# First attention: score banks 3 to 4, maxima banks 4 to 3, one exp per two score tiles

## The reference

```
def _L0_attn_ref(x, w_qkv, b_qkv, w_o, b_o):
    ...
    attn = jax.nn.softmax(jnp.einsum('blhc,bmhc->bhlm', q, k) * SCALE, axis=-1)
    heads = jnp.einsum('bhlm,bmhc->blhc', attn, v).reshape(b, l, d)
    return jnp.einsum('bld,ed->ble', heads, w_o) + b_o + x
...
    x = L0_attn_x
    xn = _layernorm(x, axis=-1)
    s = _L0_attn_ref(xn, ...)
    g = _silu(_L0_ffn_ref(xn, ...))
    x = x + s * g
```

## Time and profile before

| | us |
|---|---|
| median of 3 runs | 2436.63 |
| lowest, highest | 2425.33, 2439.51 |
| the profiled execution's own time | 2435.27 |
| its span in the trace | 2433.4 |
| first reduction of maxima to the last (L1026) | 226.8 to 1589.4 |

### The profile page before, as it was taken

How to read it: one execution, slowest core, us unless ns; L and a number is a source line. 1 busy time by engine, 2 the same in 40 slices (tenths; PEclk the granted TensorE clock), 3 DMA queues, 4 the chain that set the end, 5 groups by cost and what they waited for, 6 DMA issues and landing times. The chain is left out here.

```text
span 2433.4 us, 43647 instructions
## 1 busy us (share of the span) xinstructions
PE 2212.6 (91%) x14912; PEld 1228.7 (50%) x14912; DVE 1839.2 (76%) x3240; ACT 1442.7 (59%) x2160; POOL 462.6 (19%) x673
## 2 busy tenths in 40 slices
PE   7896899999999999999999999988999987899988
PEld 4664333333333333333333333326888876666678
DVE  5664999999999999999999999912444466888745
ACT  3443377777777777777777777772222222366743
POOL 0000000000000000000000000003545520366745
PEclk9997699999999999999999999989999999688999
DMA  6888400500500501403205002006576459766664
GB/s 206 283 288 183 53 6 6 62 6 8 62 3 13 57 3 26 44 6 44 26 3 64 6 8 62 3 3 176 154 186 157 135 190 373 170 145 146 154 164 130
DMA packets 189129, 231.90 MB, mean 95 GB/s; under 512 B 72720, under 2 KB 122768, under 8 KB 186064
## 3 DMA queue, kind: packets, MB, share of 16 engines
q1 hardware_dynamic: 176048, 210.46, 35.3%
q10 hardware_dynamic: 7184, 14.10, 2.7%
q0 software_dynamic: 5728, 5.00, 0.9%
HBM read 138.97 MB, written 89.13 MB: 94 GB/s over the span
## 5 line engine op out<-in xcount | busy, mean ns | idle before, releaser
L1026 DVE TENSOR_REDUCE a_maxes<-a_ps_a 128x2 f32<-128x1024 f32 x1024 | 1202.2, 1221 | 114.3 <-PE a_ps_a L1147 110.5
L1091 ACT ACTIVATE a_prob<-a_ps_s 128x512 f32<-128x512 f32 (+1 forms) x1376 | 1035.7, 804 | 355.2 <-PE a_ps_s L1173 349.5
L1173 PE MATMUL a_ps_s<-a_Q,a_K 50*128 50x512 f32 x2048 | 596.3, 455 | 89.8 <-ACT a_prob L1091 89.6
L1147 PE MATMUL a_ps_a<-a_K,a_Q 48*128 48x512 f32 x2048 | 551.9, 455 | 26.0 <-DMA a_Q<-s_halves 14.4
L1185 PE MATMUL a_ps_o<-a_prob,a_V 128*17 128x512 f32 x4096 | 544.9, 604 | 0.1
L1173 PEld LDWEIGHTS a_ps_s<-a_Q,a_K 50*128 50x128 f32 x2048 | 278.4, 186 | 508.7 <-ACT a_prob L1091 459.7
L1147 PEld LDWEIGHTS a_ps_a<-a_K,a_Q 48*128 48x128 f32 x2048 | 245.8, 189 | 231.5 <-issue 107.9
L984 POOL DMA_DIRECT2D a_Q<-a_m_parts x128 | 64.3, 503 | 1286.9 <-DVE a_m_parts L1018 1280.3
L1593 DVE CUSTOM_DVE_ANT_0 a_scratch<-a_ps_a,k_mask 128x256 f32<-128x256 f32 (+1 forms) x512 | 178.0, 411 | 25.9 <-PE a_ps_a L1710 24.0
L1653 ACT ACTIVATE a_prob<-a_ps_s 128x512 f32<-128x512 f32 (+1 forms) x256 | 135.6, 583 | 98.8 <-PE a_ps_s L1746 97.3
L1185 PEld LDWEIGHTS a_ps_o<-a_prob,a_V 128*17 128x17 f32 x4096 | 68.0, 95 | 150.9 <-issue 99.0
(11 more groups left out here) (195 smaller groups left out, 2260.2 us busy)
## 6 DMA issues: line engine op xcount, KB each, us to landing
s_halves<-p_parts SPq DMA_DIRECT2D x32, 512.0 KB, 5.1
s_halves<-k_K SPq DMA_DIRECT2D x32, 512.0 KB, 7.7
a_Q<-s_halves SPq DMA_DIRECT2D x186, 64.0 KB, 10.5
a_K<-s_halves SPq DMA_DIRECT2D x42, 256.0 KB, 9.0
s_xT<-p_xT SPq DMA_DIRECT2D x32, 256.0 KB, 4.0
s_cT<-p_cT SPq DMA_DIRECT2D x32, 256.0 KB, 3.7
k_wb<-s_w SPq DMA_DIRECT2D x16, 512.0 KB, 7.7
c_wb<-s_w SPq DMA_DIRECT2D x16, 512.0 KB, 8.1
```

The source lines that it names most:

```text
L1026: nc.vector.tensor_reduce(maxes[:, :, slot, qt, kc], ps_a[:, o:o + 2 * CH].rearrange("p (z k) -> p z k", z=2), AX.X, ALU.max).then_inc(a_d ...
L1091: nc.scalar.activation(prob[:, ring:ring + len(t), :].rearrange("p r q -> p (r q)"), ps_s[:, bank:bank + len(t) * CH], ACT.Exp, scale=scal ...
L1147: last = nc.tensor.matmul(ps_a[:, o + side * CH:o + (side + 1) * CH], Q[rows, q0:q0 + P], K[rows, k0:k0 + CH], start=True, stop=True)
L1173: last = nc.tensor.matmul(ps_s[:, bank + x * CH:bank + (x + 1) * CH], K[rows, k0:k0 + P], Q[rows, q0:q0 + CH], start=True, stop=True)
```

## The change

`ps_s` gets four banks and `ps_a` three. Every score step is now two tiles in two banks with one exp over 128x1024, 32 steps per iteration instead of 43. The maxima are taken in slots: an even slot is two tiles with a reduction of 128x1024, an odd slot one tile with a reduction of 128x512; an iteration has 44 slots, one of which (32) is the turn, so 21 pairs and 22 singles where there were 32 units. A slot waits for the one two before it, which used the same banks. `through(it, i)` counts the finished reductions for these waits, `slot_due` places the slots on the made-up clock by the tiles that lie before them, and the value steps are due a little later (`LAG` 30, was 24). `maxes` is now laid out in the order of the tiles. The prologue takes chunk 0 in 43 slots, and the early slots after it are 13 reductions more, with the turn between them. The copy of the output on ScalarE comes behind exp 3, which ends tile 7, where it came behind exp 2, which ended tile 4.

```
-    NJ = 2 * (TILES_IT // 3) + 1
-    NU = PAIR * TT * NCH
-    EARLY = 9
-    NPOS = NU + 1
-    TURN = NU - EARLY + 2
+    NJ = TILES_IT // 2
+    NTILES = PAIR * TT * NCH * 2
+    SLOTS = 44
+    TURN = 32
+    LAST = TURN - 3
+    EARLY = 19
+    FIRST_SLOTS = 43
...
     def tiles_of(j):
-        t = 3 * (j // 2) + (2 if j % 2 else 0)
-        return [t, t + 1] if j % 2 == 0 and t + 1 < TILES_IT else [t]
+        return [2 * j, 2 * j + 1]
...
     def clock_of(j):
-        return 12 * ((j + 1) // 2) + 7 * (j // 2)
+        return 12 * j
     ROUND = clock_of(NJ)
-    UNIT_LAG, LAG, LATE, COPY_AT = 1, 24, 1, 2
-    def unit_due(p):
-        return p * ROUND / NPOS + UNIT_LAG if p < NPOS else 2 * ROUND
+    LAG, LATE, COPY_AT = 30, 2, 3
+    def before_slot(i):
+        return 3 * (i // 2) + (2 if i % 2 else 0)
+    def bank_of(i):
+        return 2 * CH if i % 2 else 0
+    def slot_due(i):
+        return before_slot(i) * ROUND / before_slot(SLOTS) if i < SLOTS else 2 * ROUND
+    def slot_at(i):
+        first = EARLY + before_slot(i) - (2 if i > TURN else 0)
+        return 1 + first // NTILES, first % NTILES, 1 if i % 2 else 2
+    def first_slot_at(i):
+        x = before_slot(i)
+        return x, min(1 if i % 2 else 2, NTILES - x)
+    def through(it, i):
+        return (SLOTS - 1) * (it + 1) + FIRST_SLOTS - (TURN - 2) + (i if i < TURN else i - 1) + 1
...
-        maxes = n.sb("maxes", [P, 2, PAIR, TT, NCH])
+        maxes = n.sb("maxes", [P, NTILES])
-        ps_a = n.ps("ps_a", 4 * CH)
-        ps_s = n.ps("ps_s", 3 * CH)
+        ps_a = n.ps("ps_a", 3 * CH)
+        ps_s = n.ps("ps_s", 4 * CH)
...
-            def maximum(c, k, o):
-                slot, qt, kc = k // (TT * NCH), (k // NCH) % TT, k % NCH
+            def maximum(c, x, count, o, done):
...
-                dve.wait_ge(a_ready, NU * c + k + 1)
-                nc.vector.tensor_reduce(maxes[:, :, slot, qt, kc],
-                                        ps_a[:, o:o + 2 * CH].rearrange("p (z k) -> p z k", z=2), AX.X, ALU.max
+                dve.wait_ge(a_ready, done)
+                nc.vector.tensor_reduce(maxes[:, x:x + count],
+                                        ps_a[:, o:o + count * CH].rearrange("p (z k) -> p z k", z=count), AX.X, ALU.max
                                         ).then_inc(a_done, 1)
...
-            def bank_free(it, p):
-                passed_by = p - 1 - (1 if TURN <= p - 2 else 0)
-                pe.wait_ge(a_done, 2 + NU * (it + 1) + EARLY + passed_by)
+            def bank_free(it, i):
+                if it < 0 and i < TURN:
+                    pe.wait_ge(a_done, FIRST_SLOTS)
+                elif i >= 2:
+                    pe.wait_ge(a_done, through(it, i - 2))
+                else:
+                    pe.wait_ge(a_done, through(it - 1, SLOTS + i - 2))
```

More of the change, by code:

```diff
@@ L1045, in normalise, with iteration @@
                                         ).then_inc(o_done, 1)
[L1047 to L1051, removed]
+            def iteration(it, more):
+                for i in range(SLOTS):
+                    if i == TURN:
+                        split_maxima(it + 1, bank_of(i))
+                        normalise(it, bank_of(i))
                         continue
-                    step, k = unit_at(p)
+                    step, x, count = slot_at(i)
                     if step == 1 or more:
-                        maximum(it + step, k, bank_of(parity, p))
-                    if k == NU - 1:
-                        whole_maxima(it + 1)
+                        maximum(it + step, x, count, bank_of(i), through(it, i))
+                    if i == LAST:
+                        whole_maxima(it + 1, through(it, i))
             nc.vector.memset(ps_o[:], 0.0).then_inc(o_clear, 1)
-            dve.sem_inc(a_done, 2)
             dve.sem_inc(o_done, 1)
@@ L1063, in _ @@
             dve.wait_ge(router_step, 7)
[L1064 to L1069, removed]
-                else:
[L1071 to L1077, removed]
+            for i in range(FIRST_SLOTS):
+                maximum(0, *first_slot_at(i), bank_of(i), i + 1)
+            whole_maxima(0, FIRST_SLOTS)
+            for i in range(TURN - 2, SLOTS):
+                if i == TURN:
+                    split_maxima(0, bank_of(i))
+                else:
+                    maximum(1, *slot_at(i)[1:], bank_of(i), through(-1, i))
+            with dve.Fori(0, NIT - 2) as it:
+                iteration(it, True)
+            iteration(NIT - 2, False)
+            for it in (NIT - 1, NIT):
+                normalise(it, bank_of(TURN))
         @block.scalar
@@ L1130, in _, with maximum_scores @@
         def _(pe):
-            def bank_of(r, p):
-                return ((1 + r + p) % 2) * 2 * CH
-            def bank_free(it, p):
-                passed_by = p - 1 - (1 if TURN <= p - 2 else 0)
-                pe.wait_ge(a_done, 2 + NU * (it + 1) + EARLY + passed_by)
-            def maximum_scores(c, r, k, o):
-                slot, qt, kc = k // (TT * NCH), (k // NCH) % TT, k % NCH
+            def bank_free(it, i):
[5 more added lines that the diff above has]
+                    pe.wait_ge(a_done, through(it - 1, SLOTS + i - 2))
+            def maximum_scores(c, r, x, count, o):
                 half, qc = ((r // NCH) % 2) * LONG, r % NCH
-                for side in range(2):
+                for y in range(count):
+                    k, side = (x + y) // 2, (x + y) % 2
+                    slot, qt, kc = k // (TT * NCH), (k // NCH) % TT, k % NCH
                     rows = slice(side * SIDE, side * SIDE + HALF_ROWS)
@@ L1146, in maximum_scores @@
                     k0 = half + slot * T + kc * CH
[L1147 removed]
+                    last = nc.tensor.matmul(ps_a[:, o + y * CH:o + (y + 1) * CH], Q[rows, q0:q0 + P],
                                             K[rows, k0:k0 + CH], start=True, stop=True)
@@ L1190, in iteration, with slot @@
             def iteration(it, r, more, turn, before):
-                def unit(p):
-                    o = bank_of(r, p)
-                    if p == TURN:
+                def slot(i):
+                    o = bank_of(i)
+                    if i == TURN:
                         if more:
-                            bank_free(it, p)
+                            bank_free(it, i)
                         elif turn:
-                            pe.wait_ge(a_done, 2 + NU * NIT)
+                            pe.wait_ge(a_done, through(it, LAST))
                         if turn:
@@ L1220, in iteration @@
                     until = clock_of(j + 1) if j + 1 < NJ else 2 * ROUND
-                    while min(unit_due(p), values_due(v)) < until:
-                        if unit_due(p) <= values_due(v):
-                            unit(p)
+                    while min(slot_due(p), values_due(v)) < until:
+                        if slot_due(p) <= values_due(v):
+                            slot(p)
                             p += 1
@@ L1230, in iteration @@
                         v += 1
-                assert p == NPOS and v == KT - LATE
+                assert p == SLOTS and v == KT - LATE
             def turn_weights(w):
```

66 lines of the change are left out of this document (34 added, 32 removed).

## The result

The changed kernel is **slower**: 2499.51 us median (2494.99 to 2507.73, 4 runs) against 2438.07 (2425.33 to 2442.61, 4 runs), a ratio of 1.0255 with a 95% interval of 1.0226 to 1.0284. The forecast was 2502 us, range 2435 to 2540. In one of 17 later executions the kernel before took 2716.77 us at a mean granted clock of 0.729, where the others had 0.943 to 0.960, and one of 12 of an experiment did the like; the ratios leave both out.

A forecast was written before the change was run, and what follows sets the result against it. The prediction took the scores' pair bank together with the value steps in one in-order queue as the bound before. Steady iterations +66, prologue +12 and last iteration -12 gave +66 on 2436.63, so 2502 us, range 2435 to 2540.

The forecast's parts named there:

- What bounds it before: Kernel before, steady stretch: score pair bank together with value steps in one in-order queue; VectorE has slack.
- The steps: Distances between weight loads or to reductions: 1.41 us over a value step, pair bank round 1.84, single bank 1.31.
- Part 2: VectorE's reductions per iteration: 36.2 us become 36.9, so +0.8 us.
- Part 3: Maxima side, steady iterations: pair bank's 1.84 us and value steps give 44.82 us against 42.70, +2.12, or +66 us overall.
- The pattern: Repeating 12 tiles of the written order, with four pair slots, four singles, six score steps, three value steps: 8.07 us.
- Prologue: Start at half clock: pair bank takes 2.13 us per three tiles; +12 us (0 to +14).
- Last iteration: No maxima there: value steps 2.82 us apart would need some 2.1; -12 us (0 to -15).
- The faster rival: VectorE's bank round is the only limit, value steps fall into slack: 40.3 us per iteration, 2363 us; chance 12%.
- No change: Half of the value steps are covered: iteration of 42.7 us, time 2412 to 2461; chance 11%.
- Much slower: TensorE stands more and the granted clock falls to half at times: 2560 us; chance 3%.
- the score half: Score banks and exps: the wait is gone, ScalarE's 1.9 us less per iteration is off the path, worth nothing.

The follow-up runs named there:

- lighter VectorE: Every reduction of maxima over the first 256 of each tile's 512 columns, in both kernels: changed kernel 2360.83 us, kernel before 2436.08 us.
- three single banks: Changed kernel with the maxima in 64 slots of one tile, three banks in rotation: 2518.61 us, ratio to the kernel before 1.0307.
- LAG 24: Changed kernel with the value steps due a little earlier, at 24 where it has 30: 2608.36 us.
- maxima half alone: Kernel before with three maxima banks in slots of two and one, scores unchanged in three banks: 2602.69 us; with value steps due at 30, 2595.57 us.

## Why the prediction was right

- **What bounds it before** (score pair bank with value steps, VectorE with slack): VectorE's slack is shown by the lighter VectorE, which gave nothing, and TensorE's own work is ruled out by the 40.45 us of the other kernel with the same edit. That it is the score pair bank rests on the waits and on the last iteration; the one order built on it, with the value steps behind the single, failed its forecast.
- **The steps.** All were measured again after the change within 0.03 us: 1.42 and 1.40 over a value step, 1.82 for the pair bank, 1.28 for the single's. The one-bank reduction, which no row of before had, takes 0.69 us (mean 685 ns), and four in a row start (2.48 - 0.69)/3 = 0.60 apart in the run with three single banks.
- **Part 2**, +0.8 us of VectorE work: the Trainium skill's 125 ns per instruction (Perfetto Trace Analysis, section Optimizing Scalar/DVE Operations) would by estimate have put single reductions 0.53 + 0.125 = 0.66 apart, and they were 0.60 apart. This is small either way and did not carry the sum.
- **Part 3**, +2.12 us per iteration, +66: measured 44.80 - 42.67 = 2.13 at full clock. The pattern took 8.03 and not 8.07. The +68.8 of all 31 intervals hold the first, +5.0, with the early slots and the half clock in it, of which I had put the part over 2.1 to the prologue.
- **Prologue** +12: +1.3 and +9.1 up to the first chunk, and 5.0 - 2.1 = 2.9 in the first interval, 13.3 together.
- **Last iteration** -12: -14.1, in part by luck. I read 2.82 us per value step from two uneven distances, where six make 2.47, so that the fourth score bank gives 16 x (2.47 - 1.97) = 8 us and not 11. Another 4.6 us come from the half clock that the kernel before had there and the changed one hadn't. The rest isn't broken down.
- **The faster rival** (value steps fall into slack) is out: 91% of an added 0.22 us came through. *No change* likewise. *Much slower*, by a falling clock, did not happen in this kernel, but in part it did with LAG 24 and, nearly through the whole stage, in both runs with thin value steps; so 3% was perhaps a low price for it.
- **Where I was too sure**: that the score half is worth nothing. The sum needed only that it is off the path in the order of the changed kernel, and there it was right. As a statement on the half by itself it was 0.3 to 2.1 us per iteration off, depending on the order, and my walk of the maxima half alone was off too (44.5 to 46.5 against 47.7).

## What to carry to other kernels

Where one in-order queue feeds two engines out of a fixed number of PSUM banks, count for each engine what it has in store, in microseconds of its own work, and compare this with the longest thing in the queue plus the time until the next load reaches it. Giving a bank from one side to the other pays only if the giver's store still covers that; here three tiles, 1.73 us, did not cover 1.41 + 0.55 us, and the bound moved to the giver. To learn which side binds, halve one engine's work and look at the period: busy shares of 90% stood on both sides here, and the same edit was worth 4.5 us per iteration in one kernel and nothing in the other.

## What the runs showed that I had not expected

- With less work for TensorE both kernels were slower. With 15 of 16 value steps a quarter as wide, the granted clock was half for nearly the whole stage (0.50 and 0.54 in the stretch 800 to 1000 us), and the time was 2687.9 us where the changed kernel has 2499.51, and 2586.54 where the kernel before has 2438.42. These are one execution each, as said above.
- With LAG 24 the granted clock, full in the changed kernel, dipped to half for 3 to 10 us in seven iterations. In a stretch at full clock TensorE was busy 172.76 of 200 us there, where it was 180.84 in the changed kernel. That looks as if more waiting brought the dips. But the maxima half alone with LAG 30 was less busy still, 169.54 us, and its clock was full all the way from 304 to 1741 us. So it isn't TensorE's busy time over such a stretch that decides, and what does is open. The first row is LAG 24, the second the maxima half with LAG 30:

```profile
800.00:1000.00 200.00, 172.76 (x1110) 62.38 (x1102) 170.35 (x204) 137.16 (x139) 11.16 (x20) 1.00 0.17 22
```

```profile
800.00:1000.00 200.00, 169.54 (x1108) 58.99 (x1109) 171.13 (x204) 141.59 (x188) 12.68 (x23) 1.00 0.18 23
```
